# Decoder with gated cross-attention: expert weights in sixteen transfers among the keys, query weights in the first transfer, constants built elsewhere

## The reference

```python
x = x + tanh(g_xattn[0]) * L0_xattn(layernorm(x), ctx, ctx, Wq, bq, Wk, bk, Wv, bv, Wo, bo)
x = x + tanh(g_ffn[0])   * L0_ffn(layernorm(x), gate_w, w1, b1, w2, b2)        # 8 experts 128 -> 512 -> 128, gelu
x = x + tanh(g_xattn[1]) * L1_xattn(layernorm(x), ctx, ctx, mask, wq, ..., wo)
x = x + tanh(g_ffn[1])   * L1_ffn(layernorm(x), gate_W, W1, b1, W2, b2, Ws1, bs1, Ws2, bs2, route_scale)
# attention: softmax(q k^T / sqrt(8)) v, then the output projection
```

## Time and profile before

| | us |
|---|---|
| median of 3 runs | 1031.39 (1027.44 to 1034.13) |
| the profiled execution, its own time | 1031.14 |
| its span in the profile | 1029.3 |
| outside the span | 1.8 |
| PE busy | 903.9 (88%) |

### The profile page before, as it was taken

How to read it: one execution, slowest core, us unless ns; L and a number is a source line. 1 busy time by engine, 2 the same in 40 slices (tenths; PEclk the granted TensorE clock), 3 DMA queues, 4 the chain that set the end, 5 groups by cost and what they waited for, 6 DMA issues and landing times.

```text
span 1029.3 us, 32569 instructions
## 1 busy us (share of the span) xinstructions
PE 903.9 (88%) x13088; PEld 654.4 (64%) x13088; DVE 729.9 (71%) x1575; ACT 588.3 (57%) x1076; POOL 520.7 (51%) x666
## 2 busy tenths in 40 slices
PE   3887789898999898999999999999999999999974
PEld 1354467676777667677666776676666666666653
DVE  5676666877858778686876867777787878787722
ACT  1165446565575755657556575666657575756550
POOL 5544435643535455354654557666666575762202
PEclk9998889999999999999999999999999999999985
DMA  5334451222212222221655757577666666666200
GB/s 139 91 89 136 133 148 40 79 69 81 74 52 69 73 76 78 71 66 56 141 114 106 133 103 160 125 154 140 138 152 129 145 133 140 133 122 110 42 1 19
DMA packets 100290, 104.47 MB, mean 101 GB/s; under 512 B 28250, under 2 KB 93100, under 8 KB 100140
## 3 DMA queue, kind: packets, MB, share of 16 engines
q1 hardware_dynamic: 98722, 102.07, 42.6%
q10 hardware_dynamic: 1418, 0.32, 0.2%
HBM read 35.89 MB, written 0.46 MB: 35 GB/s over the span
## 4 chain that ended last, share of the span: by engine, by line
PE 57%; DVE 24%; ACT 9%; issue 7%; DMA 1%; POOL 0%; SPq 0%; ACTq 0%; POOLq 0%; DVEq 0%
DVE mx L1034 13%; PE pO L1162 13%; PE pMX L1183 10%; PE pST L1141 9%; PE pKV L1228 6%; PE pKV L1219 6%; PE pFH L1350 5%; PE pFY L1282 3%; ACT P L757 2%; DVE rden L976 2%; ACT HR L809 2%; ACT L757 2%; DVE HR L932 2%; PE pFY L1286 1%; DVE ysc L1005 1%
## 5 line engine op out<-in xcount | busy, mean ns | idle before, releaser
L1034 DVE TENSOR_REDUCE mx<-pMX 112x1 f32<-112x500 f32 x768 | 487.1, 668 | 134.1 <-PE pMX L1183 131.2
L757 ACT ACTIVATE P<-pST 125x448 f32<-125x448 f32 x768 | 389.5, 542 | 291.1 <-PE pST L1141 286.1
L1183 PE MATMUL pMX<-kop,qmax 48*112 48x500 f16 (+1 forms) x768 | 285.1, 410 | 48.3 <-DVE mx L1034 38.3
L1141 PE MATMUL pST<-qexp,kop 50*128 50x112 f16 (+2 forms) x3072 | 267.7, 216 | 21.4 <-issue 11.7
L1141 PEld LDWEIGHTS pST<-qexp,kop 50*128 50x128 f16 (+2 forms) x3072 | 184.5, 101 | 87.5 <-issue 33.2
L1162 PE MATMUL pO<-P,V 125*17 125x112 f32 x6144 | 188.8, 264 | 0.0
L1183 PEld LDWEIGHTS pMX<-kop,qmax 48*112 48x112 f16 (+1 forms) x768 | 97.7, 130 | 123.1 <-DVE mx L1034 60.2
L614 POOL CAST khi<-kfull 128x500 f16<-128x500 f32 x96 | 57.9, 603 | 206.4 <-ACT kfull L773 204.9
L1162 PEld LDWEIGHTS pO<-P,V 125*17 125x17 f32 x6144 | 138.8, 98 | 34.2 <-issue 18.7
L616 POOL TENSOR_TENSOR klo<-kfull,khi 128x500 f16<-128x500 f32 x96 | 109.0, 1135 | 7.8
L705 POOL TENSOR_TENSOR Clo<-C,Chi 128x500 f16<-128x500 f32 x93 | 105.9, 1139 | 7.5
(11 more groups left out here) (147 smaller groups left out, 1110.2 us busy)
## 6 DMA issues: line engine op xcount, KB each, us to landing
C<-in_ctxT SPq DMA_DIRECT2D x31, 750.0 KB, 5.5
kop<-maskop SPq DMA_DIRECT2D x48, 437.5 KB
kop<-khi SPq DMA_DIRECT2D x192, 62.5 KB
kop<-khi SPq DMA_DIRECT2D x96, 125.0 KB
kop<-klo SPq DMA_DIRECT2D x96, 62.5 KB
kop<-klo SPq DMA_DIRECT2D x48, 125.0 KB
maskin<-in_mask SPq DMA_DIRECT2D x8, 656.2 KB, 6.0
qexp<-qmax SPq DMA_DIRECT2D x16, 182.0 KB
```

The costliest lines, as they stand in the source:

```text
L757: nc.scalar.activation(P[0:KP, slot, h * 4 * T:(h + 1) * 4 * T], pST[0:KP, h, 0:4 * T], ACT.Exp, scale=EXP_SCALE).then_inc(exp_done, 1)
L1034: nc.vector.tensor_reduce(mx[:, s % 2, c, p:p + 1], pMX[0:T, m % 2, 0:CW], AX.X, ALU.max).then_inc(max_done, 1)
L1141: mm = nc.tensor.matmul(pST[0:keys.stop - keys.start, h, i * T:(i + 1) * T], kop[rows, b, slot, keys], qexp[rows, b, slot, :, :].rearrange ...
L1183: nc.tensor.matmul(pMX[0:T, m % 2, 0:CW], qmax[rows, b, slot, :, :].rearrange("r j q -> r (j q)"), kop[rows, b, slot, c * CW:(c + 1) * CW] ...
```

## The change

The expert weights of layer 0 are loaded expert by expert, in 16 transfers of 256 KB. SP calls `expert_weights(s, slot)` four times a step, with e = 4s + slot - 2: e = 0 to 7 are `w1a`, 8 to 15 `w2a`. So e = 0 and 1 go in step 0, 2 to 5 in step 1, 6 to 9 in step 2, 10 to 13 in step 3, 14 and 15 in step 4. Each pair has its own semaphore, waited for by PE just before the matmul that uses it. `late_loads` keeps the small tensors and the mask after step 1; `w1b` and `w2b` move from after step 2 to after step 5, and PE's wait `f2_in` from the start of step 4 to the start of step 6.

The first transfer holds `wk0` and `wq0` together (`W[:, 0:2*D]`). The query weights and biases are no longer scaled: the factor moves into `head_of`. ACT copies `wq0` over `wk0`, between its first and second `Chi`. In step -1 SP issues the keys of chunk 0 ahead of the context `C`. `late_constants` is split: `masks` in slot 5 of step -1, `output_biases` in slot 8 of step 1; the loads of `woE` and `bvE` go to slot 8 of step -1.

```diff
-            sp.dma_start(W[:, 0:D], wpack[:, 0:D]).then_inc(wk_in, 16)
+            sp.dma_start(W[:, 0:2 * D], wpack[:, 0:2 * D]).then_inc(wk_in, 16)
...
                 if s == 1:
+                    sp.wait_ge(init_w, 4)
...
-                    sp.dma_start(w1a[:, 0:E0 // 2, :], w1_0[0:E0 // 2].rearrange("e d f -> d e f")).then_inc(f_in, 16)
                     sp.dma_start(maskin[:, :], mask[0]).then_inc(mask_in, 16)
-                if s == 2:
-                    sp.dma_start(w1a[:, E0 // 2:, :], w1_0[E0 // 2:].rearrange("e d f -> d e f")).then_inc(f2_in, 16)
+                if s == 5:
                     sp.dma_start(w1b[:, :, :], w1_1.rearrange("e d f -> d e f")).then_inc(f2_in, 16)
                     sp.dma_start(w2b[:, :, :], w2_1.rearrange("(c e) f d -> (e f) c d", e=2)).then_inc(f2_in, 16)
-                if s == 3:
-                    for half in (slice(0, E0 // 2), slice(E0 // 2, E0)):
-                        sp.dma_start(w2a[:, half, :, :], w2_0[half].rearrange("e (c f) d -> f e c d", c=F0C)
-                                     ).then_inc(f3_in, 16)
+            def expert_weights(s, slot):
+
+                e = 4 * s + slot - 2
+                if 0 <= e < E0:
+                    sp.dma_start(w1a[:, e, :], w1_0[e]).then_inc(w1_in[e // 2], 16)
+                if E0 <= e < 2 * E0:
+                    e -= E0
+                    sp.dma_start(w2a[:, e, :, :], w2_0[e].rearrange("(c f) d -> f c d", c=F0C)).then_inc(w2_in[e // 2], 16)
...
+                if c == 0:
+                    act.wait_ge(init_k, 2)
+                    nc.scalar.activation(w("wk0").rearrange("d (h r p) -> d h r p", r=PR, h=2),
+                                         w("wq0").rearrange("d (r h p) -> d h r p", r=PR, h=2), ACT.Copy).then_inc(init_q, 1)
...
-                if s == 4:
-                    pe.wait_ge(f2_in, 16 * 3)
+                if s == 6:
+                    pe.wait_ge(f2_in, 16 * 2)
...
-                        if use == "y0" and s == 4:
-                            pe.wait_ge(f3_in, 32)
+                        if s == 4 or s == 5:
+                            pe.wait_ge(w2_in[int(use[1])], 32)
...
+                            if s == 3 or s == 4:
+                                pe.wait_ge(w1_in[e // 2], 32)
```

More of the change, by code:

```diff
@@ L375, in build @@
         x0_in, c0_in = sem("x0_in"), [sem(f"c0_in{c}") for c in range(CH)]
-        w_in, x_in, f_in, f2_in, f3_in, wo_in = sem("w_in"), sem("x_in"), sem("f_in"), sem("f2_in"), sem("f3_in"), sem("wo_in")
+        w_in, x_in, f_in, f2_in, wo_in = sem("w_in"), sem("x_in"), sem("f_in"), sem("f2_in"), sem("wo_in")
+        w1_in, w2_in = [sem(f"w1_in{i}") for i in range(4)], [sem(f"w2_in{i}") for i in range(4)]
         c_in = sem("c_in")
@@ L379, in build @@
         init_chi = sem("init_chi")
-        init_k, init_b, init_clo = sem("init_k"), sem("init_b"), sem("init_clo")
+        init_k, init_q, init_b, init_clo = sem("init_k"), sem("init_q"), sem("init_b"), sem("init_clo")
         chi_done = sem("chi_done")
@@ L540, in step @@
                                      ).then_inc(qexp_in[s % 2], 16)
+                expert_weights(s, 0)
+                if s == -1:
+                    key_chunk(st, 1, 0)
                 if s <= NB - 3:
@@ L548, in step @@
                 if has_k(s):
-                    key_chunk(st, 1, 0)
+                    if s >= 0:
+                        key_chunk(st, 1, 0)
+                    expert_weights(s, 1)
                     if has_q(s) and s >= 0:
@@ L564, in step @@
                     sp.dma_start(maskin[:, :], mask[(s + 3 - B) // 2]).then_inc(mask_in, 16)
+                expert_weights(s, 2)
                 if has_k(s):
                     key_chunk(st, 1, 1)
+                expert_weights(s, 3)
                 late_loads(s)
@@ L738, in early_loads @@
                                           ).then_inc(init_dma, 16)
-                if s == 0 and kt == 11:
+                if s == -1 and kt == 8:
                     act.wait_ge(init_w, 4)
@@ L745, in early_loads @@
                         act.dma_start(bvE[rows, :, :], bvc.rearrange("l g i r -> g i l r")[g]).then_inc(wo_in, 16)
+                if s == 0 and kt == 11:
                     act.wait_ge(bc_in, 16)
@@ L829, in _ @@
                 quarter = slice(32 * k, 32 * (k + 1))
-                nc.vector.memset(head_of[quarter, 0, k % 2:k % 2 + 1], 1.0).then_inc(init_h, 1)
+                nc.vector.memset(head_of[quarter, 0, k % 2:k % 2 + 1], QK_SCALE).then_inc(init_h, 1)
             for j in range(2):
-                nc.vector.memset(head_of[64 * j:64 * (j + 1), 1, j:j + 1], 1.0).then_inc(init_h, 1)
+                nc.vector.memset(head_of[64 * j:64 * (j + 1), 1, j:j + 1], QK_SCALE).then_inc(init_h, 1)
             def scaled(name, width):
@@ L877, in other_weights, with masks @@
                 split_weights(0, 1, init_c, 0)
-                dve.wait_ge(init_v, 5)
+                dve.wait_ge(init_v, 4)
                 for m in range(2):
                     split_weights(1, m, init_c, 2 + 2 * m)
-            def late_constants():
+            def masks():
+                dve.wait_ge(init_p, 12)
                 nc.vector.memset(ones[:, :], 1.0).then_inc(init_l, 1)
@@ L889, in late_constants, with output_biases @@
                 dve.wait_ge(init_l, 5)
+                for j in range(2):
+                    nc.vector.tensor_scalar(headmask[:, :, j, :], ones[:, :].rearrange("p (r q) -> p r q", r=2),
+                                            rowmask[:, j:j + 1], rowmask[:, 2:3], ALU.mult, ALU.add).then_inc(init_l, 1)
+            def output_biases():
                 dve.wait_ge(wo_in, 16 * 8)
                 dve.wait_ge(init_a, 1)
+                dve.wait_ge(init_l, 7)
                 for j in range(2):
@@ L896, in late_constants @@
                                                     bvE[:, l, r:r + 1], ALU.mult, ALU.mult).then_inc(init_l, 1)
-                    nc.vector.tensor_scalar(headmask[:, :, j, :], ones[:, :].rearrange("p (r q) -> p r q", r=2),
-                                            rowmask[:, j:j + 1], rowmask[:, 2:3], ALU.mult, ALU.add).then_inc(init_l, 1)
                 for l in range(LAYERS):
@@ L1037, in step @@
                 if s == 3:
-                    dve.wait_ge(f_in, 16 * 5)
+                    dve.wait_ge(f_in, 16 * 4)
                 for kt in range(KT):
-                    if s == 2 and kt == 2:
-                        late_constants()
+                    if s == 1 and kt == 8:
+                        output_biases()
                     if kt == 0 and has_m(s - 1):
@@ L1093, in step @@
                         low_context(0)
-                        query_weights()
+                        key_bias()
                         low_context(1)
@@ L1099, in step @@
                         other_weights()
+                        masks()
                     if has_q(s) and s + 1 >= B and kt == 2:
@@ L1188, in step @@
                 if s == 0:
-                    pe.wait_ge(init_v, 5)
+                    pe.wait_ge(init_v, 4)
                     pe.wait_ge(init_c, 6)
@@ L1192, in step @@
                     pe.wait_ge(init_l, 17)
[L1193 to L1195 removed]
+                    pe.wait_ge(f_in, 16 * 4)
+                if s == 6:
+                    pe.wait_ge(f2_in, 16 * 2)
                 def free(sem_, uses, name):
@@ L1340, in step @@
                             if s == -1:
-                                pe.wait_ge(init_b, 3)
+                                pe.wait_ge(init_q, 1)
+                                pe.wait_ge(bias_in, 16 * 5)
                             nc.tensor.matmul(pFH[:, 0:T], wq, xnqT[:, :], start=True, stop=False)
```

13 lines of the change are left out of this document (3 added, 10 removed).

## The result

The changed kernel takes 1026.95 us (median of 20 runs, 1020.17 to 1033.68), the kernel before 1031.83 (20 runs on the same chip, 1027.44 to 1037.93). The ratio is 0.9943, with a 95% interval of [0.9923, 0.9963]: about 6 us gained (the two medians differ by 4.9). The interval leaves out 1, so the kernel is faster, but by less than the 1% that the prediction said a measurement can tell. Predicted was 1016.8, 14.3 us less than before; the time is outside the range of 1009 to 1025, and over the 1021 under which the prediction saw it with a chance of 0.72. The profiled execution of the changed kernel took 1027.72 us, its span 1025.7 with a mean granted clock of 0.958 (before 1029.3, 0.968).

A forecast was written before the change was run, and what follows sets the result against it. PE bounds the steady steps; in steps 2 to 4 it waits for the shift queued behind large loads. 1031.1 less 3.0, plus 0.2, less 4.2, 6.5, 5.9 and 0.6, plus 5.7 gives 1016.8 us; range 1009 to 1025.

The forecast's parts named there:

- The start: Before the first pMX matmul: xnqT copied 2.9 us earlier, first pMX about 3.0 us earlier; bounds 1.0 to 3.5.
- Rival 4: At the start: nothing is gained because another operand is last, so 1019.8 us; chance 0.06.
- Step 1: Ten DVE instructions of output_biases ahead of maxima 16 and 17, nearly hidden: cost 0.2 us (0 to 1.0).
- Step 2: Before the first score: start at 79.5 instead of 83.00, 3.5 us gained, 2.6 of wait left, plus 0.7 of clock.
- Step 3: Wait for the shift nearly gone: 4.5 us gained (4.8 less 0.3), plus 2.0 of clock.
- Step 4: Wait for the shift gone: 2.9 us gained, plus 3.0 of clock.
- step 5: Low clock phase that follows no DMA wait: half of its 1.3 us given back, 0.6 gained.
- Step 6: New PE wait for w1b and w2b at its start, 4.0 us (3.1 to 7.2), plus 1.7 of clock: cost 5.7.
- Small transfers: The 16 expert transfers stand ahead of keys or C needed half a step later: cost nothing elsewhere.
- Rival 3: Each of 16 transfers holds up the keys behind it, 1.2 us each, 19 for all: 1036 at most; chance 0.06.
- Rival 1: Clock not given back: stalls go, low phases stay in steps 2 to 5; gain 8.0, so 1023.1 us; chance 0.22.
- Rival 2: Step 6 is free, w1b and w2b landing sooner or PE coming later: 1011.1 us; chance 0.16.

The follow-up runs named there:

- context_first: Changed kernel with the context issued ahead of the keys of chunk 0 again in step -1: 1024.99 us, ratio 0.9883 to the kernel before.
- mask_in_step2: Changed kernel with the first mask loaded behind the context in step 2 instead of after step 1: 1024.62 us, ratio 0.9901 to the kernel before.
- before_third: The kernel before, no edit, timed and profiled a third time: its profile took 1032.36 us.
- before_again: The kernel before, no edit, timed and profiled a second time: its profile took 1031.11 us.
- layer1_after_step4: Changed kernel with layer 1's two weight transfers issued after step 4 instead of after step 5: 1020.87 us, ratio 0.9856 to the kernel before.
- weights_alone: Kernel before with only the sixteen expert transfers and the new place of layer 1's weights: 1027.04 us, ratio 0.9937.
- start_alone: Kernel before with only the change's start (first transfer, ACT's copy, unscaled query weights, order of keys and C): 1031.05 us, ratio 0.9993.
- all_three: Changed kernel with layer 1's weights after step 4, context ahead of keys in step -1, mask behind context in step 2: 1012.61 us, ratio 0.9814.

## Why the prediction was wrong, point by point

By the ratio 5.9 us were gained of the 14.3 predicted. The lengths of the steps below are means over three profiles of before and two of the changed kernel. Up to the end of step 6 they give 5.4 us gained, as the ratio does. Of the 8.9 that are missing, 3.5 lie in step 2, 1.8 at the start, 1.4 in step 4, 1.2 in steps 5 and 6 together, and the rest in steps 1 and 3. Over the whole span the profiles give only 1.5 (1029.7 and 1028.2): the later steps of these two give back 3.9, which the median of 20 runs doesn't show. The second of them was also the slowest of its eight runs, 1032.67 with a median of 1029.36.

**The start** (−3.0): wrong in size. Its first half was right: `xnqT` came from 12.20 to 8.71, more than the 2.9 worked out. ACT's copy took 0.29 us, in the gap that was named for it, while POOL worked (5.82 to 6.01 and from 6.12 on); DVE's copy of the same tile beside POOL took 1.12. The Trainium skill (SBUF — State Buffer, practical consequences) says that ACT waits for no other engine, and the rows agree. The step that failed was the last, "the first `pMX` comes about 3.0 us earlier". It is 1.2, near the bound of 1.0 whose name was "C's later landing". The change issues keys ahead of C, so C goes out at 15.10, between the last two DMAs of the queries, and the last of them isn't moved until most of C is. `context_first` gives 2.7 us more, over the 1.8 that were missing. Rival 4 is not what happened: the operand that comes last is the one of before, `qlo`, but later than forecast.

**Step 1** (+0.2): not told apart. Step 1 is 25.8, 28.3 and 27.6 us in three profiles of before and 28.6 and 27.1 after.

**Step 2** (−4.2: 3.5 of wait, 0.7 of clock): the shift's landing was mis-sized, and this is the largest part of what is missing. That the mask holds the shift up was right, as `mask_in_step2` shows. SP's queue and the landing of the mask (L472) in the changed kernel:

```profile
76.09 0.59 SPq L472 DMA_DIRECT2D maskin<-in_mask  x1
...
76.80 1.47 SPq L528 DMA_DIRECT2D qexp<-ct  x2
```

```profile
DMA to landing us min/median/max: 5.2/5.2/5.2
```

The mask is issued 3.1 us after the step's start, as before (3.2), and takes 5.2 us instead of the 4.2 worked out from C's 4.4. PE starts at 81.98, 0.7 us after that landing; the forecast had it start with the landing. That was read from one coincidence, 82.97 and 83.00. In `before_third` the mask is issued at 76.47 and takes 8.2, and PE starts at 84.17, before it has landed. So the shift isn't bound to the mask's landing, but is slower beside it: from SP's issue of the shift to PE's first score it is 7.1 us behind 1.7 MB, 5.2 behind the mask and 2.6 behind neither.

Counted from the step's start the first score comes after 10.9, 11.2 and 10.5 us in the three profiles of before and after 9.0 and 10.0 in those of the changed kernel: 1.4 us gained, not 3.5. PE asks for it 1.9 us earlier, as forecast, and so it waits as long as before (4.00 and 4.99, where 2.6 was expected). The low phase at this wait lasts 10.2 us in all three profiles of before and 6.8 and 13.7 in the others, so no gain of clock shows. Step 2 is 28.2 and 31.1 us in the two profiles against 30.4, 30.7 and 30.0: 0.7 gained.

**Step 3** (−6.5): right in the number, partly by luck. A wait of at most 0.7 was expected, 0.68 and 0.51 came; the step is 5.9 us shorter. But SP issues the shift 3.2 us after the step's start (104.35), not 1.5, and it is there 2.5 us later, not 3.2 to 3.7: two errors that nearly cancel.

**Step 4** (−5.9) **and step 5** (−0.6): the wait of 2.9 has gone and the step takes the 31.1 us that were forecast. The term for the clock, "step 4 (clock 0.91) takes 37.2 against 31.0 of step 6, 6.2 more, of which 2.9 is the wait, so 3.3", was read from one execution, and so was the 1.3 of step 5; `before_again` and `before_third` have neither 37.2 nor the 31.9 of step 5. The waits recur in every profile, but what the clock costs behind one does not: by the same subtraction step 4 gives 1.8 in each of the other two, where the low phase behind the wait lasts 3.4 us instead of 6.8. The low phase in step 5, ahead of which is no such wait, is in one of the three alone. The mean of three is 35.6 for step 4: 4.5 gained, not 5.9. In step 5 there was 0.4 to be gained in the mean of three, and nothing in two of them.

**Step 6** (+5.7): right. PE waits for `w2b` for 3.27 and 3.56 us (4.0 was taken, 3.1 to 7.2 the bounds) and a low phase of 10.2 follows. Steps 5 and 6 together are 68.2 and 68.5 us in the profiles of the changed kernel and 62.9, 61.6 and 61.6 before. Between the means that is 6.3 us where 5.1 was forecast (5.7 less the 0.6 of step 5), and `layer1_after_step4` gets 6.6 of it back by the lengths of its steps. So this term was if anything too small.

**Small transfers** (0): not contradicted. The sixteen transfers landed as one 250 KB chunk does, by the DMA issues of the changed kernel:

```profile
w1a<-in_w SPq DMA_DIRECT2D x8, 256.0 KB, 3.5
w2a<-in_w SPq DMA_DIRECT2D x8, 256.0 KB, 3.1
```

Rival 3 is refuted by eight more of them at 2 us. The Trainium skill (DMA: Bandwidth & Descriptors, rules for kernel authors) asks for 1 MiB and more a DMA where bandwidth is the aim. Here the kernel with pieces of 256 KB in new places was the faster one (`weights_alone`, 0.9937): what counted was what stood ahead of a small transfer, and not the time of the 4 MB.

**Of the rivals** none is the whole answer. Rival 1, with 1023.1, is nearest by the number, and its mechanism holds in part: low phases left step 4 in both profiles, step 3 in one, where the other keeps 3.4 us of 6.8, and step 2 in none. Rival 2 is refuted by the wait at 191.67.

**What stays open.** Three low phases of 3.4 us fall in the same steps, 9, 23 and 27, in both profiles of the changed kernel; those of before have none, one and none after step 6. One of them, in the first and in the second profile of the changed kernel:

```profile
289.70:321.60 31.90, 29.17 (x460) 22.63 (x452) 23.99 (x52) 16.38 (x33) 17.05 (x25) 0.95 0.24 76
```

```profile
290.90:322.80 31.90, 29.20 (x460) 22.65 (x454) 24.02 (x52) 16.44 (x33) 17.02 (x25) 0.95 0.24 76
```

Each costs 1.2 to 1.3 us, 3.7 in all, with no wait ahead of it; step 9 takes 30.7 otherwise. Less the 0.4 that one in three profiles of before costs, they are most of the 3.9 us that the two profiles give back after step 6. The other profiles bear on this. Ten profiles of kernels with the sixteen transfers have one to four such phases each from step 7 to the last 50 us of the span, 21 in all, at changing places; the four of kernels without them (three of before and `start_alone`) have one in all. So they seem to come with the transfers, and would then be a cost that the prediction put at nothing; that isn't shown. What sets them off, long after the last of the sixteen has landed, no run tells.

## What to carry to other kernels

Before pricing a transfer that is moved, write down which large one will be issued ahead of the one that PE waits for, on any engine's queue: here C ahead of the last `qlo`, the mask ahead of `ct`, and `w2b` ahead of the first matmul of step 6. Three small edits of the order of issue brought the gain from 6 to 19 us. Loads for a later stage go out a whole step early, not just before their use. A clock cost read from one profile is an estimate with an error of its own, even behind a wait that recurs: read several profiles.

## What the runs showed of the hardware that was not expected

A transfer of 14 KB on ACT's queue is held up by one of 750 KB that SP issued 0.26 us before it: 5.5 us from its issue to the matmul, and 2.8 with C out of the way (15.36 to 20.90, and 15.35 to 18.16). The one that ACT issued 0.4 us ahead of C is not: its packets are over by 16.5 us in both kernels.

The shift, two DMAs of 1.8 KB, takes 2.4 to 2.6 us from SP's issue to PE's first score where no more than one transfer of 256 KB is issued just ahead of it (`mask_in_step2` and `all_three`, steps 2 and 3). It takes 4.6 to 5.3 behind the mask's 656 KB, and 7.0 to 7.2 behind the mask and another 1 MB.

The recorded clock and the matmuls don't agree in the first 42 us. The `pMX` matmuls of the changed kernel between 20 and 42 us, and between 240 and 280 us (count, then min/median/max in ns, first and last start); both stretches have a granted clock of 1.00 in their row:

```profile
L1201 PE MATMUL pMX<-kop,qmax x23: 415/661/664, 20.9 to 41.9; 48*112 48x500 f16 x23
...
L1201 PE MATMUL pMX<-kop,qmax x34: 373/415/415, 240.3 to 279.3; 48*112 48x500 f16 x34
```

```profile
20.00:42.00 22.00, 17.51 (x68) 6.71 (x68) 13.56 (x22) 3.23 (x5) 13.32 (x16) 1.00 0.49 123
...
240.00:280.00 40.00, 36.34 (x586) 28.28 (x585) 34.35 (x74) 22.18 (x44) 22.86 (x31) 1.00 0.24 81
```

The same matmul takes 661 ns in the one and 415 in the other, and 662 in the stretch from 46 to 60 us, whose row says 0.50. So the first steps run at the slow duration although their row says 1.00, and the moment at which this ends differs from one execution to the next of one kernel: the first `pMX` under 500 ns stands at 56.7, 41.9 and 43.7 us in the three profiles of before, and at 41.9 and 60.1 in those of the changed kernel. The length of step 1 varies between executions, too, from 25.8 to 28.6 us.
